# One-hots of the receivers' digits with the edges innermost, read by TensorE with a step of 80

## The reference, cut to what matters

```
xn = _layernorm(x)
# graph branch
x1 = rms(xn) @ W_down;  xl = x1 @ Wl;  xr = x1 @ Wr
e  = einsum(leaky_relu(xl[src] + xr[dst]), att)          # one score per edge and head
alpha = exp(e - segment_max(e, dst)) / segment_sum(...)   # softmax over the edges of a receiver
g  = segment_sum(alpha * xl[src], dst) @ W_up
# mixing branch: q, k, v from xn;  (q @ k.T * SCALE) @ v @ Wo + bo
x  = x + g + mix
# feed-forward: NVFP4 fake quantization of rows and weights, silu(gate) * up, down
return x + ffn(_layernorm(x))
```

## Time and profile before

| | |
|---|---|
| median of three runs | 997.1 us |
| profiled execution, whole | 1006.45 us |
| its span (first to last instruction) | 1004.7 us |
| TensorE busy | 899.5 us, 90% |
| VectorE busy | 874.4 us, 87% |
| ScalarE busy | 545.6 us |
| GpSimd busy | 456.6 us |

### The profile page before, as it was taken

The page is one execution under the profiler, slowest core; times in us unless marked ns, Lnnn a source line. Parts: engine busy times, 40 slices in busy tenths (PEclk is TensorE's granted clock), DMA queues, the critical chain, the costliest instruction groups (busy, mean ns, idle before and its releaser), DMA issues.

```text
span 1004.7 us, 9623 instructions
## 1 busy us (share of the span) xinstructions
PE 899.5 (90%) x2786; PEld 430.9 (43%) x2794; DVE 874.4 (87%) x1032; ACT 545.6 (54%) x1930; POOL 456.6 (45%) x503
## 2 busy tenths in 40 slices
PE   4999999899999999997899999988999669998545
PEld 3775455543344444433344444333344334443222
DVE  7998989979799999998989798888897898777997
ACT  2223123105787797787889797887894440222320
POOL 5210353245667767776777677676761000000000
PEclk9999999999999999999999999998999998999768
DMA  8204342534555333563335433349732000000012
GB/s 285 84 2 133 118 122 70 177 103 139 176 82 176 97 87 94 179 197 81 87 99 186 159 92 97 86 113 259 254 76 74 1 0 1 22 21 21 22 43 79
DMA packets 63652, 105.27 MB, mean 105 GB/s; under 512 B 29080, under 2 KB 35893, under 8 KB 63579
## 3 DMA queue, kind: packets, MB, share of 16 engines
q0 software_dynamic: 18560, 50.70, 19.2%
q1 hardware_dynamic: 45034, 53.92, 16.7%
HBM read 89.15 MB, written 12.45 MB: 101 GB/s over the span
## 4 chain that ended last, share of the span: by engine, by line
DVE 45%; ACT 26%; PE 15%; issue 10%; another core or an unknown queue 3%; DMA 1%; POOL 1%; DVEq 0%; POOLq 0%; ACTq 0%
ACT round_mem L1029 20%; PE acc L821 6%; DVE z L1510 5%; DVE turned L1508 5%; DVE acc_sb L1378 4%; PE acc L662 4%; DVE turned L1370 3%; ACT pz L1016 3%; DVE round_mem L1128 2%; DVE round_mem L1129 2%; DVE round_mem L1246 2%; DVE round_mem L1126 1%; DVE round_mem L1125 1%; PE acc L854 1%
## 5 line engine op out<-in xcount | busy, mean ns | idle before, releaser
L503 POOL DMA_INDIRECT round_mem<-msg_table,idx x352 | 339.6, 965 | 169.6 <-issue 79.6
L1029 ACT ACTIVATE round_mem<-round_mem,pz 128x65 f32<-128x65 f32 x1408 | 361.8, 398 | 52.3 <-issue 27.3
L662 PE MATMUL acc<-wslot,big_a 128*128 128x512 f32 x512 | 227.0, 604 | 14.4 <-ACT big_b L967 6.6
L1378 DVE TENSOR_REDUCE acc_sb<-round_mem 128x260 f32<-128x1820 f32 (+1 forms) x62 | 121.6, 1962 | 46.0 <-ACT round_mem L1029 29.7
L662 PEld LDWEIGHTS acc<-wslot,big_a 128*128 128x128 f32 x512 | 98.4, 193 | 141.6 <-issue 129.8
L662 PE MATMUL acc<-big_b,wslot 128*128 128x512 f32 x256 | 114.5, 608 | 8.6 <-ACT big_a L974 8.6
L662 PE MATMUL acc<-wslot,big_b 128*128 128x512 f32 x256 | 110.0, 592 | 0.0
L1016 ACT ACTIVATE pz<-z 128x7 f32<-128x7 f32 (+1 forms) x248 | 56.4, 295 | 93.6 <-DVE z L1515 70.4
L1370 DVE TENSOR_TENSOR turned<-round_mem,turned 128x1560 f32<-128x1560 f32 (+1 forms) x62 | 105.4, 1700 | 2.1
L1510 DVE TENSOR_REDUCE z<-turned 128x24 f32<-128x1560 f32 (+1 forms) x62 | 105.1, 1695 | 2.1
L1508 DVE SCALAR_TENSOR_TENSOR turned<-turned,att_sb 128x1536 f32<-128x1536 f32 (+1 forms) x62 | 103.6, 1671 | 0.0
(11 more groups left out here) (201 smaller groups left out, 1010.6 us busy)
## 6 DMA issues: line engine op xcount, KB each, us to landing
big_b<-in_x SPq DMA_DIRECT2D x18, 512.0 KB
round_mem<-msg_table,idx POOLq DMA_INDIRECT x352
out_x<-big_b SPq DMA_DIRECT2D x9, 512.0 KB
wslot<-in_wv_t SPq DMA_DIRECT2D x2, 2048.0 KB
wslot<-in_wk_t SPq DMA_DIRECT2D x2, 2048.0 KB
wslot<-in_wo_t SPq DMA_DIRECT2D x2, 2048.0 KB
wslot<-in_wq SPq DMA_DIRECT2D x2, 2048.0 KB
wslot<-in_gate_w SPq DMA_DIRECT2D x1, 2048.0 KB
```

The source lines that it names most:

```text
L503: pool.indirect_dma_start(xg[g % 4][:, j, :], None, msg_table, bass.IndirectOffsetOnAxis(idx[:, c, j0 + j:j0 + j + 1], 0)).then_inc(xg_in[ ...
L662: mm = nc.tensor.matmul(o(acc[:, n % 4, :]), a, b, start=first, stop=last)
L1029: ins = nc.scalar.activation(to[:, :, j], xg[g % 4][:, j, h * HR + 1:(h + 1) * HR], ACT.Copy, scale=pz[:, g % 2, j, h:h + 1])
L1378: nc.vector.tensor_reduce(running[c].rearrange("p (i f) -> p i f", i=2), halves_of[g % 3][:, :, :, 0:n + 1], AX.X, ALU.add).then_inc(sum_d ...
```

## The change

The one-hot tables are laid out as `(a t)`: for each value a, the 80 edges of the piece lie side by side. The compare reads the digits with a step of 1 in the innermost dimension, and in place of the row `iota_b` a table `iota_of` of 40 x 80 bf16 values, in which row a is 80 times the number a. This table is made once by 40 memsets on VectorE, behind the ten of `cap_f`, and lies in the first 1600 fp32 columns of `round_mem`, which nothing else uses until the counting is over. The copy into `iota_b` goes. TensorE's weights `hi[:, :, t]` and moving operand `lo[:, :, t]` now have a step of 80 elements (160 bytes) from column to column, where they had a step of 1.

```
-        iota_b = m_mem[0:NC, 1408:1408 + 32].bitcast(BF16)
+        iota_of = xg_mem[0:EP, 0:TP * DG_HI // 2].bitcast(BF16).rearrange("p (a t) -> p a t", t=TP)
...
-        one_hot = [(a.bitcast(BF16).rearrange("p (t a) -> p t a", a=DG_HI),
-                    b.bitcast(BF16).rearrange("p (t a) -> p t a", a=DG_LO))
+        one_hot = [(a.bitcast(BF16).rearrange("p (a t) -> p a t", t=TP),
+                    b.bitcast(BF16).rearrange("p (a t) -> p a t", t=TP))
...
                 for t in range(TP):
-                    mm = nc.tensor.matmul(hist_ps, hi[:, t, :], lo[:, t, :],
+                    mm = nc.tensor.matmul(hist_ps, hi[:, :, t], lo[:, :, t],
                                           start=(q == 0 and t == 0), stop=(q == PIECES - 1 and t == TP - 1))
...
             for c in range(C):
                 nc.vector.memset(cap_f[:, c:c + 1], float(CAPS[c]))
+            for a in range(DG_HI):
+                nc.vector.memset(iota_of[:, a, :], float(a))
...
             step(nc.vector.tensor_copy(iota_f, iota_i))
-            step(nc.vector.tensor_copy(iota_b, iota_i))
...
                     ins = nc.vector.tensor_tensor(one_hot[q % 2][i],
-                                                  digit_f[:, i, q * TP:(q + 1) * TP].unsqueeze(2).to_broadcast([EP, TP, w]),
-                                                  iota_b[0:EP, 0:w].unsqueeze(1).to_broadcast([EP, TP, w]), ALU.is_equal)
+                                                  digit_f[:, i, q * TP:(q + 1) * TP].unsqueeze(1).to_broadcast([EP, w, TP]),
+                                                  iota_of[:, 0:w, :], ALU.is_equal)
```

## The result

The changed kernel takes 1025.78 us (median of four runs, 1020.47 to 1026.53), the kernel before 997.14 us (four runs, 996.82 to 999.34). The ratio is 1.0275, 95% interval 1.0241 to 1.0308: 28.6 us slower (24.0 to 30.7 by the interval), nine times the 3.2 us of the forecast. The profiled execution of the changed kernel is its shortest one, 1020.47 us with a span of 1018.7 us; that of the kernel before is longer than its median. So the two profiles are compared stage by stage, and the end by the medians.

A forecast was written before the change was run, and what follows sets the result against it. Bound: the chain, mostly TensorE alone to 74.92, then the up weights' transfer to `weight_max(1)` at 82.94. Counting reads 3.1 us plus memsets 0.1 make 3.2 us on the median 997.1: 1000.3 us, range 996.6 to 1009.5.

The forecast's parts named there:

- The sum's largest term: TensorE's counting products, line 670: strided reads raise a pair from 26.25 to 39.2 ns, putting 3.1 us on the path.
- the same 0.98 ns: Cost per weight column of packed fp32 pairs of `lin`, taken as the price of a strided column in the counting.
- e: Extra TensorE time per counted piece of 80 pairs, forecast as 1.04 us.
- the 0.1 us for the memsets: Forty VectorE memsets at the start: first statistics 0 to 1.45 us late, mostly covered, 0.1 us taken for the path.
- The upper bound: Counting pair on TensorE: load and product one after the other, 72 columns at the same rate, 70.6 ns.
- Three pieces in front of the transfer: Pieces 0, 1 and 2 are counted before the up weights' transfer, delaying it by 3e, 3.1 us.
- four in front of the starts of the receivers: The receivers' starts are written after all four pieces, with 1.48 us to spare: 4e - 1.48, 2.7 us.
- VectorE's 12 us: Faster one-hot compares save VectorE 12.1 us over four pieces, lost in waits for TensorE and the transfer: path gain 0.
- 1.30 us of cover: VectorE's idle time before 8.83, waiting for GpSimd's first `rstd`, expected to hide the memsets' delay of 0 to 1.45 us.
- Not slower: Rival: strided counting reads fit under 26.25 ns a pair or miss it by little; 997.1 to 998.8 us, chance 34%.
- 9 ns of air: Counting pair: 40 weight columns need 17 ns at the packed rate, leaving 9 of 26.25 ns for slower reads.
- The rival that each column is dearer: Counting pairs serial or each column dearer: 1003.3 us at 50 ns a pair, 1009.9 at 70.6; chance 18%.

The follow-up runs named there:

- e1_steps: Kernel before plus thirteen series of 80 small TensorE pairs at different column steps behind its end: about 25 ns a pair at steps 1,1, 100 at 80,80.
- e3_weights_only: The change with only the high digit's one-hot (the weights) laid out edges innermost, moving operand contiguous: 997.65 us, ratio 1.0289 against the kernel before.
- e8_piece_3_only: Kernel before with strided reads in piece 3 alone, its one-hots made by compares at the old rate: 975.18 us, ratio 1.0043.
- e7_vector_less: Kernel before with the rounding of the first quarter of the gate weights replaced by one copy, a probe: 969.84 us, ratio 1.0001.
- e6_groups_of_2: Kernel before with one-hots laid out with two edges innermost, so TensorE reads with a step of 2: 997.09 us, ratio 1.0008.
- e5_more_products: Kernel before with 229 more packed pairs in front of each piece's 80, into an unused PSUM bank: 993.62 us, ratio 1.0253.

## Why the prediction was wrong

**The sum's largest term.** The step that failed is "If a strided column costs the same 0.98 ns and load and product still overlap, the pair is bound by its 40 weight columns: 39.2 ns." The second half is right: the weights bind, and load and product overlap (`e1_steps`, `e3_weights_only`). The size is not. A weight column 160 bytes from the last costs 101.6 / 40 = 2.54 ns, 2.6 times the 0.98. e is 6.03 us and not 1.04. Put into the forecast's own sum, this gives 4 x 6.03 - 1.48 + 0.1 = 22.7 us. The profile has 25.8: 4.3 more by the clock (below), 1.1 less by the earlier start, and the 0.1 us for the memsets did not appear.

**The upper bound.** The 70.6 ns rested on the same 0.98 ns, taken twice. It was no bound, since no row of the trace showed a far read at all; a price from packed fp32 rows says what more bytes cost and not what more places cost. The Trainium skill's Vector Engine (DVE) Microarchitecture Reference, section 5.2 Measured stream behaviour on trn2, gives 2.5 ns per column for VectorE with a step of 24 words. I set it aside as another engine's and kept 70.6 ns as the upper end. The measured 2.54 ns for TensorE's weights, at a step of 40 words, lies close to it, and the moving operand's 2.05 ns below; whether the two engines share a cause no run shows. The Trainium skill's rule of 16-byte lines in Advanced Engine Details and Errata, section SBUF Cachelines, had the direction right, but two places fit it badly: a step of 4 elements, with two hits in a line, already costs (40 ns a pair for 25), and a step of 80 costs more than one of 8 (100 for 76), though each has one column to a line.

**What was missing.** The clock. The prediction said nothing of it. Pieces of far reads leave TensorE at a lower granted clock, 0.58 and 0.66 in the two stretches shown behind them where it was 1.00, and unchanged transposes, projections and `lr` groups pay for it: 4.3 us in the profile of the change, 7.4 in that of `e3_weights_only`. How much falls on the lower level differs from run to run, which makes most of the difference between 25.8 us at `weight_max(1)` in one profile and 28.7 in another. The 24.0 to 30.7 us of the result's interval hold both; a closer account of the 28.6 is not shown.

**Right.** Three pieces in front of the transfer, four in front of the starts of the receivers, the later one decides, and beyond e = 1.48 us it is the second: `e8_piece_3_only`, and the missing idle time at 108.72. VectorE's 12 us bring no gain that the runs can see: `e7_vector_less`, `e6_groups_of_2`. The memsets are covered: the statistics came 0.5 us late, within the forecast 0 to 1.45, and 0.85 of the 1.30 us of cover was left. The shift goes to the rounds one for one: 25.8 at 83 us, 25.5 at the rounds. From there to the end it is shown only roughly: `e3_weights_only` has 29.4 us at `weight_max(1)`, 29.5 at the rounds and a median loss of 27.6.

**The chances.** "Not slower" had 34% on the strength of 9 ns of air and the floor of small products. The strided reads do not fit under it: a step of 2 costs nothing, a step of 4 already 15 ns a pair. The rival that each column is dearer, at 18%, had the direction, and its dearest case, 1009.9 us, was still 16 us short; its price rested on the same 0.98 ns.

## What to carry to other kernels

Before a layout is turned for the sake of one engine, look at what step the other reader gets, and price it by a trace that has such a read; rows of packed reads bound nothing. Where the reader is TensorE with products as small as these (40 and 32 columns), keep the step at 2 bf16 elements or fewer: groups of two edges gave VectorE its full rate and TensorE its old one. And ask first whose wait ends last: here VectorE waited twice for TensorE and once for a transfer that TensorE's reading releases, which said that only TensorE's order and time had a price, and moving one piece of counting and one small product there was worth 0.46% (0.26 to 0.67).

## What the runs showed of the hardware that was not expected

- A far column costs TensorE 2.54 ns as a weight (40 columns, 101.6 ns) and 2.05 ns as a moving operand (32 columns, 65.6 ns); two operands read at a time cost the larger of the two. The granted clock does not change this: 99 ns a pair at 0.50, 96 at 0.87 (`e1_steps`).
- The price does not simply grow with the step: pairs of about 25 ns at steps 1 and 2, 40 at 4, 76 at 8 and 16, 70 at 64, 100 at 80 and 81. Why 64 is cheaper than 80 stays open.
- VectorE's compare of bf16 reached two elements per step where its innermost dimension has only two elements and the digits come in runs of two (1.83 us for 3200 in `e6_groups_of_2`, 3.49 in the kernel before).
- Some 8 us of TensorE time in a piece left the clock at 1.00 behind it when filled with packed products (`e5_more_products`, pieces 0 to 2) and at 0.58 when filled with far reads (the change), though the profile has TensorE busy in both.
